# Three matmuls that nobody reads in every attention slot, one bank for the turned rows, and two gathers issued later

## What is computed

```python
c_kv = x @ W_dkv                                     # 32 latents a token
s_i = relu(einsum('bthd,bsd->bths', q_i, k_i))       # 4 index heads of 64
I = einsum('bths,h->bts', s_i, idx_w)
I = where(local, inf, I); I = where(causal, -inf, I)
_, idx = top_k(I, 96)                                # 64 of them are the local window
key_c, value = (c_kv @ W_uk)[idx], (c_kv @ W_uv)[idx]
key_r = pope((x @ W_kr)[idx], angle of the rank)     # 32 of rotary, turned by the rank
scores = (q_c . key_c + q_r . key_r) * scale         # 8 heads
out = softmax(scores) @ value
return out @ W_out
```

## Time and profile before

| | us |
|---|---|
| median of three runs | 1677.89 |
| lowest and highest | 1676.58, 1678.89 |
| the profiled execution, its own time | 1669.73 |
| its span, first to last instruction | 1667.9 |

### The profile page before, as it was taken

How to read it: one execution, slowest core, us unless ns; L and a number is a source line. 1 busy time by engine, 2 the same in 40 slices (tenths; PEclk the granted TensorE clock), 3 DMA queues, 4 the chain that set the end, 5 groups by cost and what they waited for, 6 DMA issues and landing times. The chain is left out here.

```text
span 1667.9 us, 18630 instructions
## 1 busy us (share of the span) xinstructions
PE 1243.2 (75%) x6088; PEld 820.3 (49%) x6088; DVE 777.3 (47%) x1520; ACT 731.6 (44%) x1629; POOL 543.2 (33%) x564
## 2 busy tenths in 40 slices
PE   6549959988997767157778778777868755298897
PEld 2148827744773222035546555555546543175554
DVE  2175565545543553055655555455555444013526
ACT  4713337734773542034444444444434433054425
POOL 1000000000002335716666666666666552600000
PEclk8579969986995776555565575655665565557889
DMA  5000000000001555142112222211222221100000
GB/s 170 0 1 0 0 0 1 1 0 1 1 1 57 183 191 175 41 151 44 41 26 42 43 44 42 46 42 21 44 43 42 42 39 30 25 1 26 1 0 26
DMA packets 78920, 70.23 MB, mean 42 GB/s; under 512 B 31810, under 2 KB 59140, under 8 KB 78324
## 3 DMA queue, kind: packets, MB, share of 16 engines
q1 hardware_dynamic: 62964, 52.91, 11.3%
q0 software_dynamic: 15872, 16.28, 5.2%
HBM read 44.76 MB, written 24.38 MB: 41 GB/s over the span
## 5 line engine op out<-in xcount | busy, mean ns | idle before, releaser
L605 POOL DMA_INDIRECT arena_hi<-rank_table,idx_T x256 | 248.3, 970 | 152.6 <-issue 70.7
L605 POOL DMA_INDIRECT arena_lo<-rank_table,idx_T x240 | 235.7, 982 | 164.3 <-issue 66.8
L645 PE MATMUL bank<-arena_hi 128*32 128x32 f32 (+3 forms) x1288 | 182.9, 343 | 35.1 <-issue 29.7
L645 PE MATMUL bank<-arena_hi,arena_lo 128*32 128x32 f32 (+3 forms) x864 | 142.1, 332 | 74.1 <-ACT arena_lo L1314 47.6
L618 POOL TENSOR_TENSOR arena_lo<-arena_lo 128x512 f32<-128x512 f32 x8 | 10.9, 1365 | 499.1 <-DVE arena_lo L1716 498.7
L645 PE MATMUL bank<-arena_lo 64*128 64x80 f32 (+6 forms) x376 | 115.6, 425 | 72.2 <-ACT arena_hi L1384 33.0
L645 PEld LDWEIGHTS bank<-arena_hi,arena_lo 128*32 128x32 f32 (+2 forms) x864 | 112.0, 210 | 111.2 <-ACT arena_lo L1314 53.8
L645 PEld LDWEIGHTS bank<-arena_hi 128*32 128x32 f32 (+3 forms) x1288 | 99.2, 164 | 99.1 <-issue 67.0
L645 PEld LDWEIGHTS bank<-arena_lo 64*128 64x128 f32 (+3 forms) x376 | 77.8, 265 | 128.2 <-issue 118.8
L1789 DVE SCALAR_TENSOR_TENSOR arena_lo<-arena_lo,iw 128x512 f32<-128x512 f32 (+4 forms) x114 | 75.4, 661 | 124.4 <-ACT arena_lo L1335 75.7
L1384 ACT ACTIVATE arena_hi<-bank 32x128 f32<-32x128 f32 x128 | 33.9, 265 | 209.0 <-remote 139.8
(11 more groups left out here) (260 smaller groups left out, 2544.2 us busy)
## 6 DMA issues: line engine op xcount, KB each, us to landing
rank_table<-arena_lo SPq DMA_DIRECT2D x32, 512.0 KB, 3.6
arena_lo<-q_lat SPq DMA_DIRECT2D x48, 128.0 KB
arena_hi<-rank_table,idx_T POOLq DMA_INDIRECT x256
arena_lo<-q_g SPq DMA_DIRECT2D x64, 64.0 KB
arena_lo<-rank_table,idx_T POOLq DMA_INDIRECT x240
h<-in_h SPq DMA_DIRECT2D x2, 1024.0 KB, 8.4
q_l<-arena_hi SPq DMA_DIRECT2D x8, 256.0 KB
q_g<-arena_hi SPq DMA_DIRECT2D x8, 256.0 KB, 2.7
```

The costliest lines, as they stand in the source:

```text
L605: pool.indirect_dma_start(out=G[b][:, q, :], out_offset=None, in_=rank_table[0:JG * index_width(i), :], in_offset=bass.IndirectOffsetOnAxi ...
L645: return pe.matmul(out_, lhsT, rhs, start=start, stop=stop, **kw)
```

## The change

On GpSimd, `gather(0)` is issued at the end of chunk 2 instead of chunk 1, and `gather(1)` after the last chunk instead of at the end of chunk 2. On TensorE all groups' rows are turned through bank 2, and `rows_turn(n)` waits for ScalarE's copy of the rows of group `n - 1` instead of `n - 2`. In each of the 134 slots TensorE does three further matmuls, at the top, after the scores and before the turn of the probabilities: each multiplies 128 columns of `q_split[0]` with 512 columns of `k_hi`, single pass, into bank 3, which nothing reads in these slots.

```diff
@@ -631,9 +631,11 @@
                         pool.tensor_copy(tab[b][:, :, DR:ROW], lat_rows[:, j:j + 1, :].to_broadcast([P, JG // 2, DC]))\
                             .then_inc(t_latb, 1)
-                if c in (1, 2):
-                    table_stored(pool, c)
-                    gather(c - 1)
+                if c == 2:
+                    table_stored(pool, 1)
+                    gather(0)
+            table_stored(pool, 2)
+            gather(1)
             table_stored(pool, NT)
             for i in range(EARLY, NT):
                 gather(i)
@@ -934,11 +936,11 @@
-                if n >= 2:
-                    pe.wait_ge(a_gts, n - 1)
+                if n >= 1:
+                    pe.wait_ge(a_gts, n)
                 for p in range(2):
                     pair = G[i % 2][:, 4 * g + 2 * p:4 * g + 2 * p + 2, :].rearrange("p j r -> p (j r)")
-                    last = pe.transpose(bank[2 + n % 2][:, p * P:(p + 1) * P], pair, ident[:])
+                    last = pe.transpose(bank[2][:, p * P:(p + 1) * P], pair, ident[:])
                 last.then_inc(a_gt, 1)
@@ -982,6 +984,10 @@
+            def stay_busy():
+
+                mm(bank[3], q_split[0][:, 0:P], k_hi[:, 0:C])
+
@@ -993,15 +999,18 @@
                 for s in range(SLOTS):
                     n = s - ATTN_LAG
+                    stay_busy()
                     if 0 <= n + 1 < GROUPS:
                         rows_turn(n + 1)
                     if 0 <= n < GROUPS:
                         scores(n)
+                    stay_busy()
                     if 0 <= n - 2 < GROUPS:
                         values(n - 2)
                     for i, what, k in SLOT_STEPS[s]:
                         if what == "sum":
                             index_scores(i, k)
+                    stay_busy()
                     if 0 <= n - 1 < GROUPS:
                         probs_turn(n - 1)
@@ -1356,7 +1365,7 @@
-                fn(GT[n % 2], bank[2 + n % 2][:, 0:2 * P], ACT.Copy).then_inc(a_gts, 1)
+                fn(GT[n % 2], bank[2][:, 0:2 * P], ACT.Copy).then_inc(a_gts, 1)
```

## The result

The changed kernel took 1698.84 us (median of five, 1695.30 to 1725.12) beside 1677.89 us for the kernel before on the same chip: a ratio of 1.0124 with a 95% interval of 1.0067 to 1.018. It is slower, where I had forecast 1640 us. The profiled execution is one of the longer ones, 1715.08 us, 16 us over its median, and that of the kernel before lies 8 us under its own; so the two traces show a loss of 45.4 us where the medians show 21.0.

The account below looks back on a forecast made before the run. It took TensorE at half clock to bound gather-free slots, and posts held while gathers run to lengthen the others. Terms -23 + 0 - 5 - 10 = -38 us gave a median of 1640 us from 1678, range 1550 to 1712.

Parts of the forecast that it names:

- Gathers moved, -23: Set-up and first slots: issuing the gathers of tiles 0 and 1 later saves 23 us in all.
- The opening: End of set-up: the sparse-attention slots open 26 us earlier, near 691 us, with ends of 21 and 42.
- slots that were free of gathers now meet them: First slots, beside tile 1's 32 gathers: a cost of 3 us, 0 at best, 20 if a post is held.
- One bank, 0: Turn of the rows on TensorE: the wait for ScalarE's copy is over before TensorE comes to it, 0 us.
- Fillers in slots with gathers, -10: Some 96 slots with gathers: clock 0.75 for 0.6 outweighs the extra matmuls, -10 us; ends +124 and -100.
- Fillers in the late slots, -5: Some 26 slots without gathers: extra matmuls raise the clock and save 5 us; ends +33 and -18.
- Full clock for three quarters: Slots without gathers: three quarters of the 26 reach full clock, about 2.65 us a slot, against 4.6 at half.
- the clock goes with how dense TensorE's work is: Whole kernel: clock 0.60 where TensorE is 76% busy, 0.96 where it is 95% busy.
- The slower one: Top of the slot, before the turn of the rows: extra matmuls lie on the path, 1713 us; chance 0.25.
- The "full clock" rival: All slots: full clock throughout, GpSimd becomes the bound at 40 us a tile, 1540 us; chance 0.18.
- If the slots open at 691 us and the whole is still slower, it was the fillers: Test set beforehand: an early opening with a slower total puts the loss on the extra matmuls.

Follow-up runs that it names:

- e16: Kernel before with only the two gathers moved, no extra matmuls, both banks, on a chip that holds posts: ratio 1.0004.
- e9: Changed kernel with the three extra matmuls in slots 0 to 105 only, on a chip that holds posts: 1696.21 us, ratio 1.0094 to the kernel before.
- e2: Kernel before with only one bank for the turned rows, on a quick chip: ratio 1.0002.
- e3: Kernel before with one bank and the three extra matmuls, gathers in their old place, on a quick chip: the extra matmuls cost 0.7%, 12 us.
- e7: Kernel before without the gathers of tiles 2 to 15, which attend over the rows of tiles 0 and 1, on a quick chip: 1405.81 us.
- e8: Kernel before without the gathers of tiles 2 to 15, plus one bank and the three extra matmuls, on a quick chip: 1408.27 us.
- e10: Changed kernel with six extra matmuls a slot instead of three from slot 106 on: 17 us over the changed kernel's median, one execution.
- e13: Changed kernel with only the first of the three extra matmuls, at the top of the slot, on a quick chip: ratio 0.9896 to the kernel before.
- e17: Kernel before with one bank and three extra matmuls, gathers unmoved, on a chip that holds posts: executions at 1679 and 1717 to 1722 us, beside 1656.16 to 1678.81.

## Why the prediction was wrong, by its own steps

**Gathers moved, -23.** The opening was right (28.7 us for 26). The failed term is "slots that were free of gathers now meet them": I took 3 us and an upper end of 20; 26.5 were given back by tile 0 in the kernel after, 21 in e16, and in the end the move measures nothing (1.0004, give or take 0.4%). I had named the mechanism (a post held as in rows 7) and priced it at one hold, where the unbroken stream of 40 us holds every slot beside it. On quick chips the move gives 10 to 13 us, by the medians of three runs.

**One bank, 0.** Right where it was measured by itself, on a quick chip, and no trace of the other kind has a wait that it would bring.

**Fillers in slots with gathers, -10.** The clock came as forecast (from 0.60 to 0.73 over tiles 3 to 12, I had 0.75), the time did not: +17.5 us in the kernel after, +23 in e9. The failed step is the one that lets a slot's length follow TensorE's clock at all. The earlier trace rows held the contrary: POOL's stream was 40 us of the 48.8 and its stops the rest, so the loop ran through POOL and the held posts. I reckoned with TensorE's 4.7 us of busy time as though that was the chain, and set the fillers off against its idle share. What the runs showed in its place: the fillers lengthened POOL's stops, from 87.4 to 104.0 us over tiles 3 to 12. e2 against e3 and e7 against e8 show from the other side that a higher clock does not pay for them: 13 us more, and 10.5 us more over the same seven tiles.

**Fillers in the late slots, -5.** "Full clock for three quarters" failed in the profiled execution (0.50 from 1480 to 1550 us, part of the +31.8 us of the late slots). The prices were near: at full clock 2.86 us for my 2.65, at half 4.99 for my 4.6. My sentence that the clock goes with how dense TensorE's work is was wrong too, by my own row of 39.69 us busy of 40 at 0.50. Without those fillers e9's ratio is 1.0094 for 1.0124; by these points the late slots make about a quarter of the loss, and the slots with gathers the rest, but the intervals overlap, so the shares are rough. The Trainium skill ("TensorE: Matmul & The Clock Gate", Part 1) has sustained matmul activity bring the clock up; 1480 to 1550 us, PE busy for 67.13 of 70 us at 0.50, disagrees for a stream of this make, and e10's 30.00 of 30 us at 1.00 agrees.

**The rivals.** The slower one gave 1713 us and had the sign. Its place, the top of each slot, was tested only on a quick chip (e13); what the traces show is a price paid as stops of POOL, and in late slots 1.68 us for three fillers, more than the 1.29 that it reckoned with. The "full clock" rival's end of 40 us a tile is real on another kind of chip, and not by the clock: the held posts, which I had named against it, are not there. "If the slots open at 691 us and the whole is still slower, it was the fillers" stood in the prediction and holds for the sign, by e16 and e17; but it took the 23 us of the move as kept, and they were not.

## What to carry to other kernels

Before paying work for a faster clock, find out what paces the loop with the engine's own time taken out: here 40 of 48.8 us a tile were GpSimd's issue, and no clock of TensorE could shorten those. Work that is added to lift a clock has to be paid at that clock, or at the lower one if the lift does not come; here it paid in single slots, and in no pair of runs on one chip that differ by it (and the one bank) alone. A start that is won by moving a long stream of gathers must be priced for what the stream does to the work that it now stands beside, over its whole length.

## What the runs showed of the hardware

The same program takes 10 to 11% less time on some chips than on others (1491 to 1494 us for 1666 to 1680). On the slower kind, TensorE's posts reach the other engines late while GpSimd issues indirect DMAs: copies waited up to 25.1 us on a releaser long done, all such waits of the kernel before lie between 745 and 1460 us, where its gathers of tiles 2 to 15 run, and e2_bank's trace has none. The mechanism is not known, and no run without gathers fell on such a chip. A verdict on one chip did not carry over: the move is worth 0.8 to 1.1% on three quick chips and nothing measurable on chip 12; the whole change costs 1.2% on the first chip and is not settled on the quick kind.

TensorE's clock in slots of the same make, with the same three wide matmuls and PE busy for 96% of the time and more, was seen at both levels: 0.50 over 70 us in the kernel after, 1.00 over 20 us in e8. What decides between them no run shows.
